# Eight steps moved in four hand-written instruction orders of a layer pipeline

## The chip, the cores and the metric

The kernel runs on one core of one Trainium2 chip. The metric is the time of one execution on the device in microseconds (us): the median of the runs shown, and the lowest and highest of them. One execution was also profiled. All times inside the kernel are counted from the first instruction of that profiled execution.

## The reference

16 samples x of 256 x 256 numbers (fp32) go through four layers, each of which is added to its own input:

```
x = x + (x @ W[subject] + b[subject])                      # one of 8 matrices per sample
x = x + zX*lap_x(x) + zY*lap_y(x) + zR*x*(1-x)             # reflecting borders
x = x + attention(x, side)                                 # 16 heads of 16 columns
x = x + w0*chosen(x) + w1*shared0(x) + w2*shared1(x)       # relu(x @ wi) @ wo, 256->1024->256
```

In the attention, the queries come from `side`, the keys and values from x; each query also sees its own key, and keys past the sample's length are masked. The weights w0 to w2 are a softmax over a small net that reads the first token of the three experts' outputs. `chosen` is one of three experts, by the sample's label.

## The kernel before

A turn of the main loop handles three samples at once, in different layers. In turn i, sample i goes through its linear layer, the Laplacian and the projections of the attention; sample i-1 goes through its heads; sample i-2 goes through the experts. The loop covers i = 2 to 15 (14 turns); the first two and the last two samples are written out around it. Every engine has its own order of steps as a text: `PE_BODY` for TensorE (PE), `ACT_BODY` for ScalarE (ACT), `DVE_BODY` for VectorE (DVE), `POOL_BODY` for GpSimd (POOL), `SP_BODY` for the queue that issues the DMAs. No planner sorts them: an engine does its steps in exactly this order, and waits at a semaphore where another engine isn't done. The step names that matter here:

- `S0` to `S15`: the scores of a head, for its maximum. PE multiplies (line 745), DVE takes the maximum (1148). After `S7` and `S15` DVE does six small steps on 16 columns (1155 to 1161).
- `E0` to `E15`: the scores again with the maximum taken off. PE multiplies (758) in two halves, and between them multiplies the weights of an earlier head with its values (700, 701; "attend"; head h-3 in `E`h; head 7 in `E10`, heads 8 and 9 in `E12`). ACT takes the exponential twice, in fp32 (`prob`, 984) and rounded to f16 (`prob_hi`, 988). Then DVE (heads 1, 3, 5, 7, 11, 13, 15; line 1168) or POOL (the others; 1403) subtracts the two, which gives `prob_lo`, the low part that the attend needs. There are three buffers of each, so `E`h needs the low part of head h-3.
- `H0` to `H11` and `P0` to `P11`: the first and the second matrix of the three experts in four steps each. PE multiplies, ACT rounds the hidden part (1027), DVE takes the residue (1232). After `P3`, `P7` and `P11` ACT copies one expert's output out of PSUM (1012).
- `wi0` to `wi3`, `wo0` to `wo3`: a quarter of the chosen expert's matrices, loaded by DMA into `raw`. ACT rounds it (1005), POOL takes the residue (1339).
- `x_parts`, `w_parts`, `s_parts`: the same split for the next sample, its matrix and its side input (ACT 907, 910, 913; POOL 1356). On DVE `x_parts` is a step of a few columns.
- `gate0a`, `gate0b`: the first terms of the small net, on DVE (1242, 1247).
- `x1`, `react`, `lap`, `x1_parts`, `x2_parts`: the sample after the first and second layer and its split. ACT rounds (943), DVE takes the residue (1092), which PE needs for `kp`, the keys.
- `half`: DVE sums the attends of the first eight heads from the PSUM tile `pv` (1176, twice), the denominators (1179) and their inverse (1181). Line 1179 sets the semaphore `pv_freed`; head 8's attend waits for it, since it writes over the same columns.
- `q`, `qa`, `qb`: the queries and their split into three bf16 parts (ACT 934, 937; POOL 1364).

The PSUM banks `front0` and `front1` are used in turn by the steps S, E, m, x1, q, lap, kp, ks, vs, vp and self, in PE's order (`RING`). A step waits until the step two places before it in this ring has been read: `S13` for DVE's maximum of `S12`, `E2` for ACT's exponentials of `E1`, `kp` for ACT's exponential of `E11`.

Of the kernel before, what the change touches and what calls it, by code (L numbers as in the profile page):

```python
# [55 lines left out]

PE_BODY = """
H0 H1 S0 S1 P0 S2 S3 H2 S4 S5 P1 S6 S7 H3 S8 P2 m0 H4 S9 S10 P3 S11 H5
E0 S12 P4 E1 S13 H6 E2 S14 P5 E3 S15 H7 E4 P6 E5 E6 H8 m1 E7
x1 P7 q E8 H9 E9 lap P8 E10 H10 E11 E12 kp E13 P9 E14 E15 H11 P10 pvend P11  # L60
vs aT ks gate wo logits vp self
""".split()
ACT_BODY = """
H0 wi0 H1 x3_keep wi1 H2 wi2 wi3 H3 m0 wo0 H4 wo1 x_parts P3 H5 E0 w_parts wo2 E1 H6 E2 wo3 E3 H7 E4 E5 E6 m1 H8 s_parts E7
x1_parts react P7 q E8 H9 E9 x2_parts E10 qa H10 E11 E12 kp E13 E14 E15 H11 qb kq P11
aT vs ks x3_parts logits vp x2b sum
""".split()
DVE_BODY = """
H0 S0 S1 H1 S2 S3 S4 S5 H2 S6 S7 S8 H3 S9 S10 H4 S11 gate0a H5 S12 S13 E1 S14 H6 S15 E3 H7 gate0b x_parts E5 H8
x1 E7 x1_parts react lap x2_parts half H9 E11 kp H10 E13 gate1 E15 H11  # L70
att k3 gate2 aT relu wo logits x3_parts mix scale vp self
""".split()
POOL_BODY = """
# [1408 lines left out]
```

## Time and profile before

| | |
|---|---|
| median of 3 runs | 1039.62 us (1036.63 to 1039.71) |
| the profiled execution: its time | 1038.21 us |
| its span, first to last instruction | 1036.4 us |
| busy: PE | 978.4 us (94%) |
| busy: DVE, ACT, POOL | 780.8 us (75%), 688.3 us (66%), 610.1 us (59%) |
| mean granted TensorE clock | 0.982 |
| one turn of the loop, H0 to H0 of the next turn | about 60.3 us |

A row of a timeline holds: start in us, duration in us, engine, line, operation, tile written <- tiles read, partitions x elements and types, how many instructions are merged in it, and in brackets how long the engine stood idle before and what ended that. A row of the waits holds: engine, tile and line that waited <- engine, tile and line waited for: us in total, how many times, the longest. A wait shows as a long row, not as idle time, where the instruction had already been started and then could not go on.

The turn whose rows are shown starts at 512.29 us. It is the eighth of the experts' samples (sample 7), while the heads are those of sample 8.

### The profile page before, as it was taken

Reading aid. Unit: us, or ns where it says so; the run is one execution under the profiler, and the core shown is the slowest. Engines: PE = TensorE matmul, PEld = TensorE weight load, DVE = VectorE, ACT = ScalarE, POOL = GpSimd, SP = SyncE. Lnnn points to the kernel's source line nnn. Section 1 sums busy time; section 2 is a strip of 40 time slices with the busy share of each in tenths; the row PEclk is TensorE's granted clock in tenths of the full one; section 3 lists DMA queues with packets and bytes.
Section 4 is the critical chain, followed back from the end, with each engine's and each line's share of the span. In section 5 each row is a group of like instructions: output and inputs, shape, how many; then the busy total and the mean of one; then the engine's idle time right before and its main releaser. Section 6 shows DMA issues by size and latency. Waiting matters only on the chain.

```text
span 1036.4 us, 27927 instructions
## 1 busy us (share of the span) xinstructions
PE 978.4 (94%) x9601; PEld 924.9 (89%) x9601; DVE 780.8 (75%) x1558; ACT 688.3 (66%) x1443; POOL 610.1 (59%) x546
## 2 busy tenths in 40 slices
PE   7678999999999999999999999999999999999886
PEld 6468899999999999999999999999999999999886
DVE  5657788777878878787877878787787878778633
ACT  5365876768587676858667685866768586666641
POOL 4475656566464656647565664756566475655440
PEclk9779999999999999999999999999999999999998
DMA  6716242341524244162424316242431524242110
GB/s 156 180 43 123 83 63 82 84 100 41 107 76 61 82 86 98 41 112 72 61 82 90 93 44 114 66 61 82 91 92 50 113 61 61 82 94 60 43 51 11
DMA packets 92028, 82.70 MB, mean 80 GB/s; under 512 B 12100, under 2 KB 90980, under 8 KB 92004
## 3 DMA queue, kind: packets, MB, share of 16 engines
q1 hardware_dynamic: 91572, 81.99, 34.9%
q10 hardware_dynamic: 432, 0.39, 0.3%
q8 instruction: 15, 0.25, 0.1%
q14 instruction: 9, 0.07, 0.0%
HBM read 52.59 MB, written 4.20 MB: 55 GB/s over the span
## 4 chain that ended last, share of the span: by engine, by line
PE 55%; issue 13%; DVE 8%; ACT 8%; SPq 6%; POOL 5%; DMA 4%; ACTq 0%; DVEq 0%; POOLq 0%
PE out L638 5%; PE out L640 5%; PE out L639 5%; PE front L758 5%; PE hid L638 4%; PE hid L639 4%; PE hid L640 4%; PE front L638 4%; PE front L640 4%; PE front L639 4%; DMA raw<-in_wo 3%; PE front L745 3%; ACT prob_hi L988 3%; PE pv L700 2%; PE pv L701 2%
## 5 line engine op out<-in xcount | busy, mean ns | idle before, releaser
L1403 POOL TENSOR_TENSOR prob_lo<-prob,prob_hi 128x512 f16<-128x512 f32 x144 | 175.0, 1216 | 119.2 <-ACT prob_hi L988 119.2
L638 PE MATMUL hid<-x_hi,exp_hi 128*128 128x256 f32 x768 | 230.7, 300 | 1.8 <-DVE x_lo L1228 1.8
L638 PE MATMUL out<-hid_hi,exp_hi 128*128 128x256 f32 x768 | 226.7, 295 | 1.6
L639 PE MATMUL hid<-x_lo,exp_hi 128*128 128x256 f32 x768 | 216.8, 282 | 0.0
L640 PE MATMUL hid<-x_hi,exp_lo 128*128 128x256 f32 x768 | 216.0, 281 | 0.0
L639 PE MATMUL out<-hid_lo,exp_hi 128*128 128x256 f32 x768 | 214.4, 279 | 0.0
L640 PE MATMUL out<-hid_hi,exp_lo 128*128 128x256 f32 x768 | 214.2, 279 | 0.0
L1339 POOL TENSOR_TENSOR exp_lo<-raw,exp_hi 128x512 fp32r<-128x512 f32 x128 | 169.7, 1341 | 68.6 <-ACT exp_hi L1005 68.6
L1148 DVE TENSOR_REDUCE s_max<-front 128x2 f32<-128x512 f32 x256 | 169.0, 687 | 54.2 <-PE front L745 52.5
L984 ACT ACTIVATE prob<-front 128x512 f32<-128x512 f32 x256 | 153.3, 599 | 53.3 <-PE front L758 53.3
L1027 ACT ACTIVATE hid_hi<-hid 128x512 fp32r<-128x512 f32 x192 | 114.5, 596 | 105.8 <-PE hid L640 104.0
L1232 DVE SCALAR_TENSOR_TENSOR hid_lo<-hid,hid_hi 128x512 fp32r<-128x512 f32 x192 | 130.6, 680 | 49.9 <-ACT hid_hi L1027 47.4
L638 PEld LDWEIGHTS out<-hid_hi,exp_hi 128*128 128x128 f32 x768 | 144.5, 188 | 5.8 <-issue 2.6
L638 PEld LDWEIGHTS hid<-x_hi,exp_hi 128*128 128x128 f32 x768 | 145.0, 189 | 4.5 <-DVE x_lo L1228 1.9
L639 PEld LDWEIGHTS hid<-x_lo,exp_hi 128*128 128x128 f32 x768 | 145.6, 190 | 0.0
L640 PEld LDWEIGHTS hid<-x_hi,exp_lo 128*128 128x128 f32 x768 | 145.0, 189 | 0.0
L639 PEld LDWEIGHTS out<-hid_lo,exp_hi 128*128 128x128 f32 x768 | 144.8, 189 | 0.0
L640 PEld LDWEIGHTS out<-hid_hi,exp_lo 128*128 128x128 f32 x768 | 144.2, 188 | 0.0
L988 ACT ACTIVATE prob_hi<-front 128x512 f16<-128x512 f32 x240 | 143.9, 600 | 0.0
L758 PE MATMUL front<-q_rows,k_rows 100*128 100x256 bf16 x512 | 124.8, 279 | 10.0 <-ACT prob_hi L988 5.1
L1168 DVE TENSOR_TENSOR prob_lo<-prob,prob_hi 128x512 f16<-128x512 f32 x112 | 96.2, 860 | 15.8 <-ACT prob_hi L988 14.8
L745 PE MATMUL front<-k_rows,q_rows 97*128 97x256 bf16 x512 | 88.2, 280 | 14.5 <-DMA k_rows<-x_raw 6.7
(181 smaller groups left out, 2270.1 us busy)
## 6 DMA issues: line engine op xcount, KB each, us to landing
raw<-in_wi SPq DMA_DIRECT2D x64, 256.0 KB, 3.9
raw<-in_wo SPq DMA_DIRECT2D x64, 256.0 KB, 2.8
q_rows<-w_raw SPq DMA_DIRECT2D x80, 128.0 KB, 3.6
k_rows<-x_raw SPq DMA_DIRECT2D x48, 128.0 KB, 5.5
k_rows<-x1T SPq DMA_DIRECT2D x45, 128.0 KB, 4.4
x_raw<-in_x SPq DMA_DIRECT2D x16, 256.0 KB, 2.9
w_raw<-in_w SPq DMA_DIRECT2D x16, 256.0 KB, 2.7
s_raw<-in_side SPq DMA_DIRECT2D x16, 256.0 KB, 3.7
```

What stands on the lines that cost most here:

```text
L638: nc.tensor.matmul(acc, w_hi, a_hi, start=first, stop=False)
L639: nc.tensor.matmul(acc, w_hi, a_lo, start=False, stop=False)
L640: return nc.tensor.matmul(acc, w_lo, a_hi, start=False, stop=last)
L745: last = nc.tensor.matmul(psum[:, t * S:(t + 1) * S], q_rows[0:ROWS_MAX, h, t * P:(t + 1) * P], k_rows[0:ROWS_MAX, h, :], start=True, stop ...
L758: last = nc.tensor.matmul(psum[:, k * S:(k + 1) * S], k_rows[0:ROWS_EXP, h, k * P:(k + 1) * P], q_rows[0:ROWS_EXP, h, :], start=True, stop ...
L984: last = nc.scalar.activation(prob[:, h % NPROB, :], psum[:, :], ACT.Exp, scale=SCALE)
L988: last = nc.scalar.activation(prob_hi[:, h % NPROB, :], psum[:, :], ACT.Exp, scale=SCALE)
L1027: nc.scalar.activation(hid_hi[:, s % 2, :], hid_bank[s % 2][:, :], ACT.Relu).then_inc(hid_hi_done, 1)
L1148: nc.vector.tensor_reduce(s_max[:, :, h:h + 1], psum, AX_X, ALU.max).then_inc(freed["S"], 1)
L1232: nc.vector.scalar_tensor_tensor(hid_lo[:, s % 2, :], hid_bank[s % 2][:, :], 0.0, hid_hi[:, s % 2, :].bitcast(F32), ALU.max, ALU.subtract) ...
L1339: nc.gpsimd.tensor_tensor(lo, source, hi.bitcast(F32), ALU.subtract).then_inc(w_split, 1)
L1403: nc.gpsimd.tensor_tensor(prob_lo[:, h % NPROB, :], prob[:, h % NPROB, :], prob_hi[:, h % NPROB, :], ALU.subtract).then_inc(prob_split_poo ...
```

## The change

PE does `E5` before `P6` rather than after it. ACT copies the first expert's output (`P3`) before it rounds `wo1` and `x_parts`; it does `qa` before `E10` rather than after it, and `E11` before `H10`. DVE takes the maximum of `S12` before the residue of `H5`; behind `lap` it does `H9`, then `half`, then `x2_parts`, where it did `x2_parts`, `half`, `H9`. POOL's and SP's orders, the written-out opening and every instruction itself stay as they are; the order within the ring of banks stays too.

```diff
--- before.py
+++ after.py
@@ -56,18 +56,18 @@
 
 PE_BODY = """
 H0 H1 S0 S1 P0 S2 S3 H2 S4 S5 P1 S6 S7 H3 S8 P2 m0 H4 S9 S10 P3 S11 H5
-E0 S12 P4 E1 S13 H6 E2 S14 P5 E3 S15 H7 E4 P6 E5 E6 H8 m1 E7
+E0 S12 P4 E1 S13 H6 E2 S14 P5 E3 S15 H7 E4 E5 P6 E6 H8 m1 E7
 x1 P7 q E8 H9 E9 lap P8 E10 H10 E11 E12 kp E13 P9 E14 E15 H11 P10 pvend P11
 vs aT ks gate wo logits vp self
 """.split()
 ACT_BODY = """
-H0 wi0 H1 x3_keep wi1 H2 wi2 wi3 H3 m0 wo0 H4 wo1 x_parts P3 H5 E0 w_parts wo2 E1 H6 E2 wo3 E3 H7 E4 E5 E6 m1 H8 s_parts E7
-x1_parts react P7 q E8 H9 E9 x2_parts E10 qa H10 E11 E12 kp E13 E14 E15 H11 qb kq P11
+H0 wi0 H1 x3_keep wi1 H2 wi2 wi3 H3 m0 wo0 H4 P3 wo1 x_parts H5 E0 w_parts wo2 E1 H6 E2 wo3 E3 H7 E4 E5 E6 m1 H8 s_parts E7
+x1_parts react P7 q E8 H9 E9 x2_parts qa E10 E11 H10 E12 kp E13 E14 E15 H11 qb kq P11
 aT vs ks x3_parts logits vp x2b sum
 """.split()
 DVE_BODY = """
-H0 S0 S1 H1 S2 S3 S4 S5 H2 S6 S7 S8 H3 S9 S10 H4 S11 gate0a H5 S12 S13 E1 S14 H6 S15 E3 H7 gate0b x_parts E5 H8
-x1 E7 x1_parts react lap x2_parts half H9 E11 kp H10 E13 gate1 E15 H11
+H0 S0 S1 H1 S2 S3 S4 S5 H2 S6 S7 S8 H3 S9 S10 H4 S11 gate0a S12 H5 S13 E1 S14 H6 S15 E3 H7 gate0b x_parts E5 H8
+x1 E7 x1_parts react lap H9 half x2_parts E11 kp H10 E13 gate1 E15 H11
 att k3 gate2 aT relu wo logits x3_parts mix scale vp self
 """.split()
 POOL_BODY = """
```

## Rows read from the trace of the kernel before

**Rows 1.** Waits of PE in the whole trace: two of the longest groups.
```profile
PE pv L700 <- DVE den L1179: 7.6, 14, 0.5
...
PE front L745 <- DVE s_max L1148: 5.6, 15, 0.5
```

**Rows 2.** Timeline of PE: last of P3; first of S13, E2, head 3's attend.
```profile
528.00 0.28 PE L640 MATMUL out<-hid_hi,exp_lo 128*128 128x256 f32 x1
...
532.38 0.39 PE L745 MATMUL front<-k_rows,q_rows 97*128 97x256 bf16 x2 [0.34 <-DVE s_max L1148]
...
534.04 0.40 PE L758 MATMUL front<-q_rows,k_rows 100*128 100x256 bf16 x2
...
540.42 0.19 PE L700 MATMUL pv<-v_cols,prob_hi 128*128 128x49 bf16 x1
```

**Rows 3.** Timeline of ACT: wo1, x_parts, P3; last of E1.
```profile
528.25 0.63 ACT L1005 ACTIVATE exp_hi<-raw 128x512 fp32r<-128x512 f32 x1 [0.17 <-DMA raw<-in_wo]
528.79 0.61 ACT L907 ACTIVATE x_hi<-x_raw 128x512 fp32r<-128x512 f32 x1
529.30 0.64 ACT L1012 ACTIVATE e_out<-out 128x256 f32<-128x256 f32 x2
...
532.94 0.62 ACT L988 ACTIVATE prob_hi<-front 128x512 f16<-128x512 f32 x1
```

**Rows 4.** Timeline of POOL: x_parts, wo1, E0; wo2; wo3, E4.
```profile
529.48 1.28 POOL L1356 TENSOR_TENSOR x_lo<-x_raw,x_hi 128x512 fp32r<-128x512 f32 x1 [0.51 <-ACT x_hi L907]
530.72 1.33 POOL L1339 TENSOR_TENSOR exp_lo<-raw,exp_hi 128x512 fp32r<-128x512 f32 x1
532.02 1.16 POOL L1403 TENSOR_TENSOR prob_lo<-prob,prob_hi 128x512 f16<-128x512 f32 x1
...
534.38 1.74 POOL L1339 TENSOR_TENSOR exp_lo<-raw,exp_hi 128x512 fp32r<-128x512 f32 x1
...
537.20 1.28 POOL L1339 TENSOR_TENSOR exp_lo<-raw,exp_hi 128x512 fp32r<-128x512 f32 x1
539.91 1.17 POOL L1403 TENSOR_TENSOR prob_lo<-prob,prob_hi 128x512 f16<-128x512 f32 x1 [1.43 <-ACT prob_hi L988]
```

**Rows 5.** Timeline of DVE: S12; E1; first small step behind S15; E3.
```profile
531.64 0.68 DVE L1148 TENSOR_REDUCE s_max<-front 128x2 f32<-128x512 f32 x1
...
533.59 1.38 DVE L1168 TENSOR_TENSOR prob_lo<-prob,prob_hi 128x512 f16<-128x512 f32 x1
...
537.52 0.99 DVE L1155 SCALAR_TENSOR_TENSOR s_max<-s_max,s_self 128x16 f32<-128x16 f32 x1
...
539.23 0.68 DVE L1168 TENSOR_TENSOR prob_lo<-prob,prob_hi 128x512 f16<-128x512 f32 x1
```

**Rows 6.** Timelines of DVE and of POOL, first loop turn, behind S7.
```profile
98.94 2.22 DVE L1155 SCALAR_TENSOR_TENSOR s_max<-s_max,s_self 128x16 f32<-128x16 f32 x1
...
97.36 3.77 POOL L1339 TENSOR_TENSOR exp_lo<-raw,exp_hi 128x512 fp32r<-128x512 f32 x3
```

**Rows 7.** Timeline of PE: end of head 7's attend, start of head 8's, kp.
```profile
552.01 0.18 PE L701 MATMUL pv<-v_cols,prob_lo 128*128 128x49 bf16 x1
...
554.62 0.18 PE L700 MATMUL pv<-v_cols,prob_hi 128*128 128x49 bf16 x1 [0.55 <-DVE den L1179]
...
555.05 0.39 PE L638 MATMUL front<-x_hi,lin_hi 128*128 128x256 f32 x1
```

**Rows 8.** Timelines of DVE (x2_parts, half), ACT (E11), POOL (E9, E10).
```profile
552.00 1.46 DVE L1092 TENSOR_TENSOR x_lo<-react,x_hi 128x512 fp32r<-128x512 f32 x1 [0.70 <-ACT x_hi L943]
553.38 1.01 DVE L1176 TENSOR_REDUCE att<-pv 128x128 f32<-128x384 f32 x2
...
554.39 0.61 ACT L984 ACTIVATE prob<-front 128x512 f32<-128x512 f32 x1
...
551.74 1.17 POOL L1403 TENSOR_TENSOR prob_lo<-prob,prob_hi 128x512 f16<-128x512 f32 x1
553.58 1.16 POOL L1403 TENSOR_TENSOR prob_lo<-prob,prob_hi 128x512 f16<-128x512 f32 x1 [0.67 <-ACT prob_hi L988]
```

## The prediction

> **What bounds the kernel now.** I read the page first (its table stands above): PE is busy for 978 of 1036 us, and no other engine comes near. A change of order can therefore only give back the gaps of PE. Next I read PE's waits [rows 1]: of those that come back in every turn, two stand out, head 8's attend waiting for the denominators of `half` (14 times) and the scores of `S13` waiting for a maximum (15 times). They are small in that view because it counts a gap only from the modelled end of the matmul before it. Start against start they are larger: `S13` begins at 532.38 [rows 2], though PE had nothing to do between `E1` and it, whose two matmuls begin at 531.65; I put its undisturbed start at 531.88, so 0.50 us are lost. Head 8's attend begins at 554.62 with 0.55 us of idle time before it [rows 7], about 0.7 us from start to start. Together 1.2 us of a turn of 60.3 us. Then I read the timelines of the other engines around the two places, since the question of such a change is what is late next.
>
> **The first place: S12, P3, E5.** DVE takes S12's maximum from 531.64 to 532.32 [rows 5], behind H5's residue, and S13 follows 0.06 us later. With `S12` ahead of `H5` it comes over 1 us earlier, and the 0.50 us of S13 are gone. The next wait is that of `E2`, which takes the bank of `E1`. ACT's last exponential of E1 ends at 532.94 + 0.62 = 533.56 [rows 3]. The three moved steps of ACT take the same time in either order, and H5 behind them starts only when PE has ended it, so I keep the 533.56. With 0.05 us to the matmul, E2 begins at 533.61 instead of 534.04 [rows 2]: 0.43 us gained, not 0.50. What PE and ACT do after that shifts by 0.43 us.
>
> Now the price. `P3` can't start on ACT before PE's last matmul of it ends, at 528.00 + 0.28 = 528.28 [rows 2]. So it starts at 528.32, where `wo1` started at 528.25 once its DMA had landed [rows 3]. From start to start P3 takes about 0.54 us and wo1 too (528.25 to 528.79). So ACT's `x_parts` starts at 529.40 rather than 528.79, and POOL's, which waited 0.51 us for it, at 530.09 rather than 529.48 [rows 4]: 0.61 us later. `wo1` was to hand long before on POOL but stands behind it. From there to the end of `wo3` POOL has no gap: x_parts, wo1, E0, w_parts, wo2, E2, wo3, with only 0.04 us of overlap between neighbours. It ended at 537.20 + 1.28 = 538.48 [rows 4]; DVE's E1 holds it up once, before and after. One step of 1.33 falls back to 1.28, so it ends about 0.57 us later, at 539.05. That costs nothing by itself, since POOL then had 1.43 us of idle time ahead of E4 [rows 4].
>
> But DVE's small steps behind S15 and its E3 sit in this gap. Line 1155 starts at 537.52 and takes 0.99 us for 16 columns [rows 5]. It ends at 538.51, 0.03 us behind POOL's wo3. The same instruction took 2.22 us where three POOL steps followed each other [rows 6]. So I read it as held until POOL's instruction has ended. E1 on DVE is the same case (1.38 us, where E3 takes 0.68 us) [rows 5], and wo2 on POOL the reverse (1.74 instead of 1.28 us) [rows 4]: the two engines take turns, with whole instructions. E3 started 0.72 us behind the end of line 1155. In the new order 1155 ends at 539.08, if it is held through wo3, and E3 can begin at 539.80; if it slips in between POOL's E2 and wo3, as E1 does between its neighbours, line 1157 is held in its place, and E3 begins at 539.57. POOL's `E4`, however, follows PE and ACT, and comes 0.43 us earlier: 539.91 - 0.43 = 539.48. It gets there first in both cases, by 0.32 or 0.09 us. It holds DVE until 539.48 + 1.17 = 540.65, and E3 ends 0.55 us later (E1 ended at 534.97, POOL's step ahead of wo2 at 534.38 + 0.04), at 541.20. Head 3's attend needs exactly this residue and stood at 540.42 [rows 2]. It would now come at 541.27: 0.85 us later than before, where without the jam it would come 0.41 us earlier.
>
> The Trainium skill (SBUF — State Buffer, Who interferes with whom) says that a DVE instruction with two SBUF inputs contends with a GpSimd instruction that reads SBUF, and that whichever issues first has the shared ports for the whole instruction while the other is fully blocked. By that rule E4 wins as above; were the port shared by bandwidth instead, E3 would be stretched by some tenths and most of the 0.41 us kept. The trace agrees in the blocking but not in who goes first: line 1155 at 98.94 was older than the last of the three POOL steps and still came behind it [rows 6].
>
> `E5` ahead of `P6`: PE's work is the same. Head 2's attend moves 1.5 us forward and now comes about 0.1 to 0.2 us behind its residue from POOL (E2, two steps ahead of wo3 in the row above): no wait, but no room either. ACT's exponentials of E5 and E6 get room. I count this as nothing, as x1, two steps on in the ring, takes the bank of `m1`, and m1 stays behind H8. The cost if head 2's cover is gone is at most POOL's delay of 0.57 us, less the room; it would then stand in for a part of the wait at head 3, not add to it. `gate0a` is no longer held, and P4 needs P3's copy earlier than before: a few hundredths in turns in which wo1's DMA is late.
>
> **The second place: half, E11, qa.** PE ends head 7's attend at 552.01 + 0.18 = 552.19 [rows 7]. `half` starts at 552.23 instead of 553.38 [rows 8], and the 0.7 us of head 8's attend are gone. Next is `kp`, at 555.05 [rows 7], with two needs. One is the bank of E11: ACT ends that exponential at 554.39 + 0.61 = 555.00 [rows 8], and kp follows by 0.05 us. Ahead of H10's rounding, E11 waits for PE only; I put it at 554.08, so kp may start at 554.74, 0.31 us earlier. The other is `x2_parts` on DVE, now behind half. Half takes 1.29 us to the start of the next step (two sums of 1.01 us together, two small steps), so x2_parts starts at 553.52. POOL's E10 starts at 553.58 [rows 8]. Now it is DVE that is first, by 0.06 us; x2_parts then takes the 0.69 us of an instruction that is not held (it took 1.46 us behind POOL's E9, which ended 0.55 us before it did) [rows 8] and is there at 554.21. So I take 0.31 us of gain. The other end of the range: POOL first, x2_parts ends at 553.58 + 1.16 + 0.55 = 555.29, and kp is 0.30 us later than before. `qa` ahead of E10 fills time in which ACT waits for PE (POOL and SP do nothing with it earlier, as their orders are unchanged): nothing. No DMA is moved, and SP's queue waits for nothing new.
>
> **The sum.** + 0.85 - 0.31 = + 0.54 us in each of the 14 turns of the loop, + 7.6 us. The written-out turns have no next sample to split or no experts and get nothing from me. Against the profiled execution's own 1038.21 us (1.8 us more than its span) this gives 1045.8 us; the median of the runs is 1.4 us above it, so for the median I say 1047.2 us.
>
> **The rivals.** (1) Faster: E3 gets ahead of E4. That takes 0.1 to 0.3 us in a chain of a dozen steps that I carried along, or ports that let DVE's queue through between its small steps. Then head 3's attend is on time: - 0.41 - 0.31 = - 0.72 us a turn, - 10.1 us: 1029.5 us. For it speaks that both waits that the change is aimed at are real and fall away; against it the full row of POOL. (2) Slower still: the jam at head 3, and x2_parts behind E10 as well. The point is the 0.06 us by which x2_parts is first. + 0.85 + 0.30 = + 1.15 us a turn: 1055.7 us. (3) About even: only about half the turns are jammed, as DMA landings and exponentials differ by some hundredths from turn to turn: (0.85 - 0.41) / 2 - 0.31 = - 0.09 us a turn, 1038.3 us; or no jam at head 3 but one at kp, - 0.11 us a turn, 1038.1 us. That the order isn't carried out as written is ruled out, since the texts are the program.
>
> **How the numbers follow.** The forecast, 1047.2 us, gets 0.48, with a range of its own of 1043 to 1051 (E3's end is good for 0.2 us a turn to either side). Rival 1 gets 0.24, rival 2 0.12, rival 3 0.16. A measurement of this kernel can tell about 0.3%, 3.1 us, from no change; so slower is 0.48 + 0.12 = 0.60, same 0.16, faster 0.24. With the forecast, rival 3 and rival 1 (down to 1028) the range leaves out 0.12.
>
> **What would show it.** In the waits, DVE den and s_max as releasers of PE must be gone. Right: a new wait of head 3's attend for DVE's prob_lo, over 1 us, in nearly every turn; DVE's E3 row 1.3 us or longer, ending 0.55 us behind POOL's E4; kp about 0.3 us nearer to E10. Wrong: E3 with 0.68 us, and a turn of 59.6 us. If x2_parts' row is over 1.3 us and PE waits for it at kp, it is rival 2.

## The result, and the profile after

| | before | after |
|---|---|---|
| median of 6 runs | 1038.97 us (1036.63 to 1040.73) | 1045.59 us (1044.43 to 1047.68) |
| ratio to before, 95% interval | | 1.0067 [1.0051, 1.0083] |
| the profiled execution: its time, its span | 1038.21 us, 1036.4 us | 1044.43 us, 1042.6 us |
| mean granted TensorE clock | 0.982 | 0.983 |
| one turn of the loop (mean of turns 2 to 14) | 60.29 us | 60.76 us |

The changed kernel is 0.7% slower, 1.6 us below the forecast of 1047.2 us. The page of the profile shows how little the sums of busy time say of it: PE is busy for 3.3 us more, DVE for 1.0 us less, and POOL for 20 us more although it does the same instructions.

```profile
PE 981.7 (94%) x9601; PEld 927.9 (89%) x9601; DVE 779.8 (75%) x1558; ACT 688.1 (66%) x1443; POOL 630.1 (60%) x546
```

The waits of PE and of its weight loads (PEld) in the whole trace of after. They answer to [rows 1]: `den` is gone as a releaser, `s_max` has fallen from 5.6 to 0.9 us, and a new one has come, an attend that waits for DVE's low part of a head. It stood at 1.8 us in 2 waits before.

```profile
PE pv L700 <- DVE prob_lo L1168: 16.6, 14, 1.6
...
PE front L745 <- DVE s_max L1148: 0.9, 4, 0.3
...
PEld front L638 <- ACT prob L984: 4.7, 14, 0.3
```

The timeline of PE in after: the start of the turn, S13, E2, head 3's attend; then head 8's attend and kp. It answers to [rows 2, 7]. Times "into the turn" below are differences to the first row of such a timeline, as 534.07 - 514.48 = 19.59 for S13.

```profile
514.48 0.37 PE L638 MATMUL hid<-x_hi,exp_hi 128*128 128x256 f32 x1
...
534.07 0.38 PE L745 MATMUL front<-k_rows,q_rows 97*128 97x256 bf16 x2
...
535.81 0.39 PE L758 MATMUL front<-q_rows,k_rows 100*128 100x256 bf16 x2
...
543.57 0.20 PE L700 MATMUL pv<-v_cols,prob_hi 128*128 128x49 bf16 x1 [1.25 <-DVE prob_lo L1168]
...
557.09 0.19 PE L700 MATMUL pv<-v_cols,prob_hi 128*128 128x49 bf16 x1
...
557.91 0.39 PE L638 MATMUL front<-x_hi,lin_hi 128*128 128x256 f32 x1
```

Both waits of before are gone: no bracket stands behind S13 and none behind head 8's attend. The only bracket among these rows is the 1.25 us at head 3. ACT's timeline shows the moved step, P3 ahead of wo1 and x_parts [rows 3]:

```profile
530.58 0.66 ACT L1012 ACTIVATE e_out<-out 128x256 f32<-128x256 f32 x2 [0.40 <-PE out L640]
531.13 0.64 ACT L1005 ACTIVATE exp_hi<-raw 128x512 fp32r<-128x512 f32 x1
531.65 0.63 ACT L907 ACTIVATE x_hi<-x_raw 128x512 fp32r<-128x512 f32 x1
```

POOL's timeline answers to [rows 4]: x_parts, wo1, E0, w_parts, wo2, E2, wo3, E4, and, far behind, E10.

```profile
532.36 1.30 POOL L1356 TENSOR_TENSOR x_lo<-x_raw,x_hi 128x512 fp32r<-128x512 f32 x1 [1.29 <-ACT x_hi L907]
533.61 1.29 POOL L1339 TENSOR_TENSOR exp_lo<-raw,exp_hi 128x512 fp32r<-128x512 f32 x1
534.86 1.17 POOL L1403 TENSOR_TENSOR prob_lo<-prob,prob_hi 128x512 f16<-128x512 f32 x1
535.99 1.75 POOL L1356 TENSOR_TENSOR p_lo<-w_raw,p_hi 128x512 fp32r<-128x512 f32 x1
537.69 1.29 POOL L1339 TENSOR_TENSOR exp_lo<-raw,exp_hi 128x512 fp32r<-128x512 f32 x1
538.92 1.17 POOL L1403 TENSOR_TENSOR prob_lo<-prob,prob_hi 128x512 f16<-128x512 f32 x1
540.05 1.29 POOL L1339 TENSOR_TENSOR exp_lo<-raw,exp_hi 128x512 fp32r<-128x512 f32 x1
541.64 1.16 POOL L1403 TENSOR_TENSOR prob_lo<-prob,prob_hi 128x512 f16<-128x512 f32 x1 [0.30 <-ACT prob_hi L988]
...
556.76 1.59 POOL L1403 TENSOR_TENSOR prob_lo<-prob,prob_hi 128x512 f16<-128x512 f32 x1 [0.66 <-ACT prob_hi L988]
```

DVE's timeline: the six small steps behind S15, then E3 (0.68 us); and x2_parts. It answers to [rows 5, 8].

```profile
539.26 0.87 DVE L1155 SCALAR_TENSOR_TENSOR s_max<-s_max,s_self 128x16 f32<-128x16 f32 x1
540.16 1.21 DVE L1157 TENSOR_SCALAR m_parts<-s_max 128x16 bf16<-128x16 f32 x1
541.41 0.17 DVE L1158 SCALAR_TENSOR_TENSOR m_rest<-s_max,m_parts 128x16 f32<-128x16 f32 x1
541.50 0.17 DVE L1159 SCALAR_TENSOR_TENSOR m_parts<-s_max,m_parts 128x16 bf16<-128x16 f32 x1
541.70 1.12 DVE L1160 SCALAR_TENSOR_TENSOR m_parts<-m_rest,m_parts 128x16 bf16<-128x16 f32 x1
542.75 0.16 DVE L1161 SCALAR_TENSOR_TENSOR d_self<-s_self,s_max 128x16 f32<-128x16 f32 x1
542.84 0.68 DVE L1168 TENSOR_TENSOR prob_lo<-prob,prob_hi 128x512 f16<-128x512 f32 x1
...
556.72 0.63 DVE L1092 TENSOR_TENSOR x_lo<-react,x_hi 128x512 fp32r<-128x512 f32 x1
```

Lay the two timelines beside each other. A small step takes 0.17 us where no POOL instruction runs beside it. Three of them are long, and each ends within 0.05 us of the end of a POOL instruction: 1155 at 540.13 (POOL's E2 at 540.09), 1157 at 541.37 (wo3 at 541.34), 1160 at 542.82 (E4 at 542.80). So DVE's six steps take 3.58 us, from 539.26 to 542.84, and head 3's residue is there at 543.52. PE's attend starts 0.05 us later. Before the change only the first of the six was held, and from its end at 538.51 the other five took 0.72 us to the start of E3 at 539.23 [rows 5]. DVE is never idle in that view and never "waits": the wait stands in the length of the rows.

In the loop the pattern has two exceptions. The first turn has its queues later by itself (E3 ahead of E4, head 3's attend at 30.30 us into the turn, 30.20 before), and in the turn that starts at 332.94 DVE slips by. DVE's timeline of that turn (1160, 1161, E3):

```profile
360.14 0.17 DVE L1160 SCALAR_TENSOR_TENSOR m_parts<-m_rest,m_parts 128x16 bf16<-128x16 f32 x1
360.24 0.17 DVE L1161 SCALAR_TENSOR_TENSOR d_self<-s_self,s_max 128x16 f32<-128x16 f32 x1
360.32 0.68 DVE L1168 TENSOR_TENSOR prob_lo<-prob,prob_hi 128x512 f16<-128x512 f32 x1
```

and POOL's (E4):

```profile
360.30 1.73 POOL L1403 TENSOR_TENSOR prob_lo<-prob,prob_hi 128x512 f16<-128x512 f32 x1 [0.52 <-ACT prob_hi L988]
```

Here E4 came 0.20 us later into the turn than in the shown one (27.36 against 27.16). DVE was already in 1161, E3 followed at once, and POOL was held: 1.73 us. The attend started at 361.06, 28.12 into the turn, and that turn took 59.88 us, where the other twelve of turns 2 to 14 took 60.82 to 60.85. So 12 of the 14 turns of the loop are jammed.

### The profile page after: what moved, and what is told of

Same layout as the page of the kernel before. It is cut to its first block, busy times and chain, and to the rows that moved or that the text cites. A ratio compares the mean times of both kernels' runs of the same rounds, so it can differ in the third digit from the quotient of the medians.

```text
span 1042.6 us, 27927 instructions
## 1 busy us (share of the span) xinstructions
PE 981.7 (94%) x9601; PEld 927.9 (89%) x9601; DVE 779.8 (75%) x1558; ACT 688.1 (66%) x1443; POOL 630.1 (60%) x546
## 4 chain that ended last, share of the span: by engine, by line
PE 80%; DVE 8%; issue 4%; ACT 2%; SPq 2%; DMA 2%; POOL 1%; DVEq 0%; ACTq 0%; POOLq 0%
PE hid L638 8%; PE out L638 8%; PE hid L639 8%; PE hid L640 8%; PE out L640 8%; PE out L639 8%; PE front L758 5%; PE front L745 5%; PE front L638 5%; PE front L640 4%; PE front L639 4%; PE pv L700 2%; PE pv L701 2%; DVE m_parts L1157 2%; DVE s_max L1148 1%
## 5 line engine op out<-in xcount | busy, mean ns | idle before, releaser
L1403 POOL TENSOR_TENSOR prob_lo<-prob,prob_hi 128x512 f16<-128x512 f32 x144 | 187.1, 1300 | 88.8 <-ACT prob_hi L988 88.8
L1339 POOL TENSOR_TENSOR exp_lo<-raw,exp_hi 128x512 fp32r<-128x512 f32 x128 | 163.1, 1289 | 70.3 <-ACT exp_hi L1005 70.2
L700 PE MATMUL pv<-v_cols,prob_hi 128*128 128x49 bf16 x1024 | 81.9, 186 | 17.6 <-DVE prob_lo L1168 16.6
```

The lines of the kernel that those rows point to most:

```text
L700: nc.tensor.matmul(acc, prob_hi[:, h % NPROB, at:at + P], v_cols[:, k, h, :], start=(k == 0), stop=False)
L1339: nc.gpsimd.tensor_tensor(lo, source, hi.bitcast(F32), ALU.subtract).then_inc(w_split, 1)
L1403: nc.gpsimd.tensor_tensor(prob_lo[:, h % NPROB, :], prob[:, h % NPROB, :], prob_hi[:, h % NPROB, :], ALU.subtract).then_inc(prob_split_poo ...
```

## The experiments

My theory: P3's move makes POOL's row of steps end later, E4 comes earlier, and so it starts ahead of DVE's E3 and holds it, which delays head 3's attend; the second place gives 0.3 us back. The rivals: that something else in the change costs (E5's move and its cover, `half` and what stands behind it), or that the late row on POOL costs by itself, whatever E4 does. All edits are changes of one or two of the order texts; "into the turn" is the mean of turns 2 to 14. Each ratio is to runs of the kernel before that were taken beside it, whose medians lie between 1036.70 and 1039.52 us; so from one experiment to another compare the ratios and the turns, not the times.

**P3 back behind x_parts**, from the changed kernel:

```diff
 ACT_BODY
-... H4 P3 wo1 x_parts H5 ...
+... H4 wo1 x_parts P3 H5 ...
```

> The changed kernel with one of its moves undone: ACT rounds wo1 and x_parts ahead of P3 again. My theory (jam): the copy of P3 ahead of the two roundings sends POOL's row of work 0.6 us later, so that DVE's small steps behind S15 end behind the arrival of POOL's E4, and head 3's attend waits 1.3 us. Without it POOL ends wo3 about 26.2 us into the turn, DVE's E3 starts at 26.9, ahead of E4 at 27.2, and both gains stay: 0.43 + 0.31 us in each of 14 turns, less a jam of 1.3 us in one or two turns in which wo1's DMA lands latest. Ratio to the kernel before 0.990 to 0.994. Rival A (E5 ahead of P6 pulls the attends of heads 2 and 3 forward of their residues): nothing changes, 1.006 to 1.008. Rival B (S12 ahead of H5 overloads DVE): the same, 1.006 to 1.008.

Measured: 1026.98 us, 0.9904 [0.9887, 0.9920]. POOL's wo3 ends 26.17 us into the turn (26.86 in after), E3 starts at 26.75 with E4 at 27.18 behind it, head 3's attend at 27.70 (29.09 in a jammed turn of after). The turn is 59.40 us. The whole loss of the change, and a gain of 1% that it hid, hang on this one move.

**wo3 behind E4 on POOL**, the move of P3 kept:

```diff
 POOL_BODY
-... wo2 E2 wo3 E4 E6 ...
+... wo2 E2 E4 wo3 E6 ...
```

> The changed kernel with all its moves, and one more: POOL takes the residue of head 4 (E4) ahead of wo3. My theory: POOL's row then ends with E2, 25.6 us into the turn, and stands idle until E4 at 27.2; the small steps and E3 of DVE fall into this gap, E3 starts at about 26.4 and takes 0.68 us. Head 3's attend is on time, a turn takes about 59.5 us, ratio 0.988 to 0.992. Rivals A and B: the attend of head 3 stays late, since neither PE's order nor DVE's is touched; ratio 1.005 to 1.008.

Measured: 1027.05 us, 0.9905 [0.9889, 0.9922], a turn of 59.40 us. The late step is still late, but it no longer stands between the small steps and E3. DVE's timeline in this run (1155, E3; the turn starts at 506.48):

```profile
531.24 0.86 DVE L1155 SCALAR_TENSOR_TENSOR s_max<-s_max,s_self 128x16 f32<-128x16 f32 x1
...
532.81 0.69 DVE L1168 TENSOR_TENSOR prob_lo<-prob,prob_hi 128x512 f16<-128x512 f32 x1
```

and POOL's (E2, E4, wo3):

```profile
530.90 1.17 POOL L1403 TENSOR_TENSOR prob_lo<-prob,prob_hi 128x512 f16<-128x512 f32 x1
533.62 1.16 POOL L1403 TENSOR_TENSOR prob_lo<-prob,prob_hi 128x512 f16<-128x512 f32 x1 [1.55 <-ACT prob_hi L988]
534.74 1.47 POOL L1339 TENSOR_TENSOR exp_lo<-raw,exp_hi 128x512 fp32r<-128x512 f32 x1
```

1155 is held by E2 only. Then POOL is idle, the other small steps and E3 run through, and E4 finds nobody. Two different edits that keep DVE's E3 ahead of E4 give the same time.

**wo3 ahead of E1 on ACT**, to tell a late row on POOL from the order of arrival. ACT does E1, H6 and E2 one step later, which delays PE and with it E4, and POOL's row stays late:

```diff
 ACT_BODY
-... wo2 E1 H6 E2 wo3 E3 H7 ...
+... wo2 wo3 E1 H6 E2 E3 H7 ...
```

> The changed kernel, and ACT rounds wo3 ahead of E1. POOL's row stays as late as in the changed kernel (end of wo3 26.9 us into the turn), but E1's exponentials, E2 and with them POOL's E4 come about 0.5 us later (27.7 instead of 27.2). My theory, as mended by the run with P3 alone (it is the order of arrival of E3 and E4 that decides; E3 is ready at 27.4): E3 goes first and ends at 28.06, head 3's attend at 28.2, a turn takes about 59.9 us, ratio 0.994 to 0.998, faster than the changed kernel though ACT's step is only delayed. Rival C (a late row of POOL is enough by itself): head 3's attend at 29.1 or later, ratio 1.007 or over.

Measured: 1034.49 us, 0.9950 [0.9934, 0.9967]. The turn shown starts at 508.27. DVE (1157, 1160, E3):

```profile
533.94 1.21 DVE L1157 TENSOR_SCALAR m_parts<-s_max 128x16 bf16<-128x16 f32 x1
...
535.48 0.17 DVE L1160 SCALAR_TENSOR_TENSOR m_parts<-m_rest,m_parts 128x16 bf16<-128x16 f32 x1
...
535.66 0.68 DVE L1168 TENSOR_TENSOR prob_lo<-prob,prob_hi 128x512 f16<-128x512 f32 x1
```

POOL (wo3, E4):

```profile
533.83 1.28 POOL L1339 TENSOR_TENSOR exp_lo<-raw,exp_hi 128x512 fp32r<-128x512 f32 x1
535.96 1.40 POOL L1403 TENSOR_TENSOR prob_lo<-prob,prob_hi 128x512 f16<-128x512 f32 x1 [0.85 <-ACT prob_hi L988]
```

wo3 ends 26.83 us into the turn, as late as in after (26.86), and 1157 is held by it for the same 1.21 us. But E4 now comes at 27.69, E3 has gone at 27.37, and it is POOL that waits (1.40 us). The attend starts at 28.21 and the turn is 59.89 us. Letting E1, H6 and E2 wait for one more step made the changed kernel 1.2% faster; a late row alone doesn't cost what the change lost.

**The parts, from the kernel before.** S12 alone:

```diff
 DVE_BODY
-... S11 gate0a H5 S12 S13 ...
+... S11 gate0a S12 H5 S13 ...
```

> The kernel before with one move: DVE takes the maximum of S12 ahead of the residue of H5. My theory: S13's wait is gone, E2 waits for E1's exponentials instead, 0.43 us a turn are gained; POOL ends wo3 as before, so E3 is on time but for the one or two turns with the latest DMA landing of wo1. Ratio 0.995 to 0.997. Rival B (this move overloads DVE and makes E3 late): head 3's attend is over 1 us late in every turn, ratio over 1.008.

Measured: 1030.24 us, 0.9932 [0.9916, 0.9949], better than the range that I expected: the turn is 59.69 us, 0.60 less. Of this 0.50 us stands at kp (42.83 to 42.33; I had counted 0.43), and 0.1 us more comes between kp and P11, which I had not counted. S13 is at 19.64, E2 at 21.34 (21.82 before), E3 at 26.78 and E4 at 27.18, so no turn is jammed. The 0.4 us between them is enough.

S12 and P3:

```diff
 ACT_BODY
-... H4 wo1 x_parts P3 H5 ...
+... H4 P3 wo1 x_parts H5 ...
 DVE_BODY
-... S11 gate0a H5 S12 S13 ...
+... S11 gate0a S12 H5 S13 ...
```

> The kernel before with two moves: S12 ahead of H5 on DVE, and P3 ahead of wo1 and x_parts on ACT. My theory: these two are the jam; head 3's attend comes 29.1 us into the turn, x1 0.9 us later than before, a turn takes 61.2 us, ratio 1.011 to 1.013. Rival A (E5 ahead of P6 is needed for it): ratio under 0.998.

Measured: 1050.82 us, 1.0118 [1.0095, 1.0141], attend at 29.09, turn 61.10 us. As expected.

P3 alone:

```diff
 ACT_BODY
-... H4 wo1 x_parts P3 H5 ...
+... H4 P3 wo1 x_parts H5 ...
```

> The kernel before with one move: ACT copies P3 ahead of wo1 and x_parts. My theory (the jam needs both, a late row of POOL and an early E4): POOL ends wo3 at 26.9 instead of 26.3, but its E4 stays at about 27.6, so DVE's E3 starts ahead of it, at about 27.4 instead of 27.0, and ends in time for head 3's attend. Ratio 0.998 to 1.002. Rival C (a late row of POOL is enough by itself): head 3's attend over 0.8 us later, ratio over 1.008.

Measured: 1049.83 us, 1.0122 [1.0102, 1.0143]. This was a clear miss. I had thought that E4 comes early only where S12's maximum does, and had tied that to S12's move. DVE's timeline shows otherwise (the turn starts at 517.42): `gate0a`, H5's residue, S12's maximum, and, further on, 1160 and E3.

```profile
534.37 0.34 DVE L1242 TENSOR_SCALAR gate_terms<-gate,e_out 128x256 f32<-128x256 f32 x1
535.74 0.69 DVE L1232 SCALAR_TENSOR_TENSOR hid_lo<-hid,hid_hi 128x512 fp32r<-128x512 f32 x1 [1.02 <-ACT hid_hi L1027]
536.35 0.68 DVE L1148 TENSOR_REDUCE s_max<-front 128x2 f32<-128x512 f32 x1
...
544.65 1.15 DVE L1160 SCALAR_TENSOR_TENSOR m_parts<-m_rest,m_parts 128x16 bf16<-128x16 f32 x1
...
545.80 0.68 DVE L1168 TENSOR_TENSOR prob_lo<-prob,prob_hi 128x512 f16<-128x512 f32 x1
```

POOL in the same turn (E4):

```profile
544.61 1.16 POOL L1403 TENSOR_TENSOR prob_lo<-prob,prob_hi 128x512 f16<-128x512 f32 x1 [0.32 <-ACT prob_hi L988]
```

`gate0a` reads P3's output. With P3's copy early it runs in 0.34 us; where the copy comes later it meets POOL's x_parts, and takes 0.93 to 0.94 us. Then DVE is free when H5's rounding is done, and S12's maximum starts at 18.93 us into the turn, 0.42 us earlier than before (531.64 - 512.29 = 19.35, [rows 5]). In the same turn S13 starts at 19.67 and E4 on POOL at 27.19. So P3's move by itself makes both halves of the jam, the late row on POOL and the early E4; S12's move on top of it changes nothing (1.0118 against 1.0122).

**E5 back behind P6**, from the changed kernel:

```diff
 PE_BODY
-... E4 E5 P6 E6 ...
+... E4 P6 E5 E6 ...
```

> The changed kernel, with E5 behind P6 on PE again. By my count the move of E5 is worth nothing: head 3's attend at 29.1 us, x1 at 31.8 us, ratio 1.005 to 1.009, the same as the changed kernel. Rival A (E5's early place makes the attends of heads 2 and 3 late): under 0.998.

Measured: 1044.64 us, 1.0064 [1.0038, 1.0090], attend 29.10, x1 31.87, turn 60.85 us. That is after's time. With the jam in place the move is worth nothing and costs nothing; alone, without the jam, it was not run.

**half ahead of x2_parts alone**, from before:

```diff
 DVE_BODY
-... lap x2_parts half H9 E11 ...
+... lap H9 half x2_parts E11 ...
```

> The kernel before with one move: DVE does H9 and half ahead of x2_parts, ACT's order untouched. By my step for kp, the bank of E11 holds kp at 555.05 whatever DVE does: head 8's attend comes 0.7 us earlier, kp not at all. Ratio 0.998 to 1.002, waits of PE at head 8's attend gone, a wait for ACT's exponential at kp in its place. Rival D (the wait at head 8 is the whole cost): 0.7 us a turn, ratio 0.990.

Measured: 1038.62 us, 1.0023 [1.0012, 1.0034]; the top of what I had expected is just under the measured value. Head 8's attend comes 0.75 us earlier (42.40 to 41.65), but kp only 0.03 us (42.83 to 42.80), and the turn is 60.24 us against 60.29. The wait has only changed its name. Waits of PE in this run:

```profile
PE front L638 <- ACT prob L984: 6.6, 14, 0.5
```

The 0.2% that it lost can't come from the loop, which is 0.05 us a turn shorter. In its trace the written-out turn behind the loop takes 56.76 us (55.48 before) and what follows 47.11 (46.45): 1.9 us more, which goes with the granted clock there (see the end of the next section).

**half and E11**, from before:

```diff
 ACT_BODY
-... E10 qa H10 E11 E12 ...
+... E10 qa E11 H10 E12 ...
 DVE_BODY
-... lap x2_parts half H9 E11 ...
+... lap H9 half x2_parts E11 ...
```

> As the last one, and ACT's exponential of E11 ahead of H10's rounding (qa stays behind E10). By my step kp gains 0.31 us a turn: ratio 0.994 to 0.997. If qa ahead of E10 were needed for it: 0.998 to 1.001.

Measured: 1033.59 us, 0.9963 [0.9951, 0.9975]; kp at 42.47, turn 59.86 us. `half` alone gained nothing, together with E11's move it gains, and `qa`'s move isn't needed. E11's move without `half` was not run.

**x2_parts last but late**, from the changed kernel, to see rival 2 of the prediction with POOL's E10 first:

```diff
 DVE_BODY
-... lap H9 half x2_parts E11 ...
+... lap half H9 x2_parts E11 ...
```

> The changed kernel, but DVE does H9 behind half, so that x2_parts starts about 0.55 us later and behind POOL's E10. By the same rule x2_parts is then held until E10 has ended and 0.55 us on (row of about 1.2 us), kp comes 0.6 us later than in the changed kernel, and DVE's E11 and kp behind it may lose another half microsecond. Ratio 1.014 to 1.022. If the order of arrival doesn't matter (the row only shifts by 0.55 us with its 0.63 us, and kp has 0.5 us of room): 1.006 to 1.010.

Measured: 1054.23 us, 1.0137 [1.0120, 1.0154]. It is slower as expected, but just short of my range, since the second half of the delay that I expected didn't come. The turn shown starts at 521.70; POOL (E10), then DVE (x2_parts):

```profile
563.99 1.16 POOL L1403 TENSOR_TENSOR prob_lo<-prob,prob_hi 128x512 f16<-128x512 f32 x1 [0.67 <-ACT prob_hi L988]
```

```profile
564.49 1.20 DVE L1092 TENSOR_TENSOR x_lo<-react,x_hi 128x512 fp32r<-128x512 f32 x1
```

x2_parts starts 0.50 us behind E10, ends 0.54 us behind E10's end (565.69 against 565.15), and kp is at 44.06 us, 0.71 us later than in after.

**A version that beats both.** If P3's place costs through x_parts on POOL, x_parts should go first of the three on ACT, since wo1 waits there for its DMA [rows 3], and P3's copy for PE:

```diff
 ACT_BODY
-... H4 P3 wo1 x_parts H5 ...
+... H4 x_parts P3 wo1 H5 ...
```

> The changed kernel, but ACT's order around P3 is x_parts, P3, wo1. x_parts needs neither PE's P3 nor wo1's DMA, so POOL can start its row at 16.6 us into the turn, right behind wo0, and end wo3 at about 26.0 us. E3 is ready long before E4; all gains stay. Ratio 0.988 to 0.992, at least as good as with P3 put back.

Measured: 1028.20 us, 0.9880 [0.9863, 0.9896]. wo3 ends at 25.82, E3 starts at 26.57, E4 at 27.25; attend 27.77, turn 59.47 us. On top of it E11 goes ahead of H10 on PE, as it does on ACT already:

```diff
 PE_BODY
-... E10 H10 E11 E12 kp ...
+... E10 E11 H10 E12 kp ...
```

> As the last one, and PE does E11 ahead of H10, so that kp finds E11's bank read when PE gets there. kp follows E12 with no wait, about 0.35 us a turn more than in the last kernel, of which the low part of E11 may take back 0.1 us at E14: ratio 0.983 to 0.988, the fastest of all.

Measured: 1024.82 us, 0.9852 [0.9836, 0.9869], 1.5% faster than before and, by the two ratios, 2.1% faster than the changed kernel. POOL's timeline (x_parts; the turn starts at 506.80) shows no wait ahead of x_parts, which starts 16.64 us into the turn instead of 17.19 [rows 4] or 17.88:

```profile
523.44 1.28 POOL L1356 TENSOR_TENSOR x_lo<-x_raw,x_hi 128x512 fp32r<-128x512 f32 x1
```

kp comes at 41.65 us, 0.42 us earlier than without the second edit. Only 0.1 us of a turn is left of that (59.36 against 59.47 us). The lead lasts until P10 (47.47 against 47.87 us); it is lost ahead of P11 (50.01 against 50.14), where PE now waits for DVE's residue of H11. The waits of PE in this run show it, and those of the run without the second edit don't:

```profile
PE out L638 <- DVE hid_lo L1232: 4.1, 14, 0.3
```

How the two kernels stand to each other can't be told well, as their intervals overlap.

## Why the prediction was right

The forecast came out by its own mechanism, and nearly by its own numbers. Point by point (the first four in us into the turn):

| | before | predicted | after, shown turn |
|---|---|---|---|
| S13 | 20.09 | 19.59 | 19.59 |
| E2 | 21.75 | 21.32 | 21.33 |
| end of POOL's wo3 | 26.19 | 26.76 | 26.86 |
| head 3's attend | 28.13 | 28.98 | 29.09 |
| from head 3's attend to kp | 14.63 | 14.32 | 14.34 |

- **The waits aimed at** are gone, and what came next was named: E2 is bound by E1's exponential, kp by E11's. The weight load of kp still waits for ACT's `prob` in 14 cases, 4.7 us in all. (It is `prob` and not `prob_hi` because head 11 is an exception: ACT takes its exponential once, and DVE rounds it.)
- **The price of P3's place**: ACT's x_parts and with it POOL's came later by the working of the prediction, 0.69 us on POOL where 0.61 was worked out (17.88 against 17.19). The gapless row carried it to wo3, and it ended 0.67 us later instead of 0.57. Who was held up within the row was not as I wrote: w_parts took the 1.75 us beside DVE's E1, not wo2, since E1 came earlier too.
- **The jam**: E4 came 0.46 us earlier into the turn (27.62 to 27.16; predicted 0.43), ahead of E3. Here the prediction had the right result with one wrong form. It said that E3's own row would be 1.3 us or longer and end 0.55 us behind E4. In the shown turn the row has 0.68 us. The one that was held is 1160, two steps ahead; 1161 and E3 then had to follow, and E3 ends 0.72 us behind E4 (543.52 against 542.80). These 0.72 us, where 0.55 were predicted, less the 0.04 us by which E4 ended earlier still, are why the attend is 0.11 us later than predicted (it also followed E3 by 0.05 us instead of 0.07); wo3's 0.1 us has no part in it, as E4 ends after it. The branch of 1155 was the second of the two that were named: it slipped in between POOL's E2 and wo3, and 1157 was held through wo3.
- The held step is 1160 in nine turns, 1161 in two, and in one turn (start 575.32) E3 itself, which is exactly the predicted form. DVE's 1160, 1161 and E3:

```profile
602.54 0.18 DVE L1160 SCALAR_TENSOR_TENSOR m_parts<-m_rest,m_parts 128x16 bf16<-128x16 f32 x1
602.63 0.17 DVE L1161 SCALAR_TENSOR_TENSOR d_self<-s_self,s_max 128x16 f32<-128x16 f32 x1
602.72 1.66 DVE L1168 TENSOR_TENSOR prob_lo<-prob,prob_hi 128x512 f16<-128x512 f32 x1
```

POOL's E4 in that turn:

```profile
602.62 1.20 POOL L1403 TENSOR_TENSOR prob_lo<-prob,prob_hi 128x512 f16<-128x512 f32 x1 [0.45 <-ACT prob_hi L988]
```

- There E3 ends 0.56 us behind E4 (604.38 against 603.82). The cost is the same, since the attend stands at 29.11. As a sign the form of E3's row was a poor choice: 0.68 us, which the shown turn has, was half of what the prediction named as its sign of being wrong. The other half, the turn of 59.6 us, is what tells.
- **x2_parts** was to win by 0.06 us and won by 0.04 (556.72 against POOL's 556.76), with 0.63 us for the row, and POOL took the hold: 1.59 us. Rival 2's point was that close. The order H9, half decides it, as the run with x2_parts late shows.
- **E5's move** was worth nothing, as counted.
- **The sum**: predicted + 0.54 us in each of 14 turns. A jammed turn has + 0.54 us (60.83 - 60.29), but only 12 are jammed. The free one has - 0.46 (59.88 against 60.34), the first - 0.23 (62.02 against 62.25). From H0 to H0 over the loop that makes + 5.9 us instead of + 7.6. The written-out turn behind the loop has + 0.61 us, where the prediction had nothing, and the tail behind the last H0 - 0.32. Together 6.2 us, the difference of the two profiled executions (1044.43 - 1038.21). The forecast's 7.6 us for the loop was thus 1.7 too high, through the two turns that were not jammed; the end gave 0.3 us of that back by luck. Between the medians it is 6.6 us. The other 0.65 us of the distance to 1047.2 come from the starting point, the median of three runs (1039.62), where six give 1038.97.
- **Rival 1** (E3 ahead) is what single turns show, and all turns of the runs with P3 back or wo3 behind E4. Its time, 1029.5 us, is 0.990 of the median that it started from, and they gave 0.9904 and 0.9905. The prediction had said that 0.1 to 0.3 us in the chain would bring it; in the trace E4 at 27.31 us into the turn still held E3, and E4 at 27.36, 0.20 us later than in the shown turn, did not.
- **What the prediction didn't see** is that P3's move did both halves. It wrote of `gate0a` only that it "is no longer held", and credited all of E2's 0.43 us to S12's move. For the whole change that made no difference; for the parts it led to the miss of the run with P3 alone. S12's move alone would have been better than the whole change: 0.9932.

The Trainium skill (SBUF — State Buffer, Who interferes with whom) says that a DVE reduction never contends on trn2, while instructions with two SBUF inputs, and the forms of `tensor_scalar` that use the shared ports, do. The traces here agree: the maxima out of PSUM (1148) keep their 0.68 us beside POOL's steps, while 1155, 1157 and 1160 are held with 16 columns each. All these maxima read PSUM, though, so no run here tells whether it is the reduction or its source that keeps them free.

The end of the kernel differs between the runs by its granted clock. In the written-out turn behind the loop, every profiled execution takes 51.4 to 51.9 us from H0 to the first matmul of `ak_hi` into `pv` (line 638), at a granted clock of 0.99 to 1.00. The rest of that turn takes 3.85 us in before, 3.86 with x2_parts late and 3.87 with E5 back behind P6, all three at 1.00. In every run with a lower clock there it is longer: 4.33 us in after (0.62), and 5.10 us with `half` alone (0.50, the lower of the clock's two levels, 1.2 GHz). PE had stood idle for 1.24, 0.26 and 0.61 us just before, in the trace of before and in that of `half` alone alike. The stretch behind the last H0 goes the same way: 44.84 us at 0.94 (E5 back), 46.13 at 0.91 (after), 46.45 at 0.88 (before), 47.11 at 0.86 (`half` alone). Both stretches together differ by up to 3.8 us between executions (100.5 us with E5 back, 104.3 with `half` and E11). That is half of what the whole change was forecast to cost, so small effects are better read from the turn than from the total. Whether an order of steps makes the clock fall there, or chance, is open: each of these is one execution.

## What to carry to other kernels

A reordering is not paid only in waits of the engine that bounds the kernel: follow each moved step through the queue of every engine that depends on it, down to the place where two engines hold each other up, and ask who comes first there after the change. Here 0.6 us of lateness on POOL and 0.5 us of earliness on PE and ACT, both harmless alone or wanted, crossed at one point and cost 1.4 us in 12 of 14 turns, which was more than all the gains together. Run the parts alone before the whole: here `half` gained nothing without E11, and S12, which gains alone, gained nothing on top of P3.

## What the runs showed of the hardware

- **A step that is held waits for the end of the other engine's instruction, however small it is itself.** A `TENSOR_SCALAR` of 16 columns took 1.21 us and a `SCALAR_TENSOR_TENSOR` of 16 columns 1.12 us beside POOL's, 0.17 us alone. No idle time stands before it in the trace: to find such holds, look for rows of one shape with two lengths, as 0.17 and 1.21, 0.68 and 1.66 (DVE), 1.16 and 1.40 to 1.73 (POOL).
- **The order of arrival is decided within hundredths.** POOL's E4 held the next DVE step when its recorded start was 0.06 us ahead (541.64 and 541.70). With 0.01 us ahead (602.62 and 602.63) it let 1161 through and held only E3, 0.10 us behind it; with 0.02 us ahead (360.30 and 360.32) E3 ran free and POOL was held; with DVE 0.04 us ahead (556.72 and 556.76) POOL was held too. So a recorded start that is 0.01 or 0.02 us ahead doesn't say who goes first. The price of losing was 0.6 to 1.0 us for DVE (x2_parts 1.20 instead of 0.63, 1157 1.21 instead of 0.17) and 0.2 to 0.6 us for POOL.
- **Between two queues that are both full the engines took turns**, mostly: 1155 got in between POOL's E2 and wo3, where the same line in [rows 6] was held through the rest of one POOL step and the whole of the next. What tells the two cases apart wasn't tried.
